# Gelu as a tanh of its cube, its products on GpSimd, normalisations on GpSimd, one list of steps

## The reference

```python
x = L0_attn_x                                    # (8, 1024, 256)
x = x + 0.5 * ffn(layernorm(x))
x = x + attn(layernorm(x))
x = x + 0.5 * ffn(layernorm(x))
# ffn:  16 heads of 16: softmax(q k^T / 16) v, then
z = l2_normalize(z @ Wo)
z = l2_normalize(z @ Wff)
z = gelu(z)                                      # approximate=False
# attn: 8 heads of 32, linear: (q k^T) v without a softmax, then @ w_o.T + b_o
```

## Time and profile before

| | |
|---|---|
| median of 3 runs | 3022.5 us (3019.59 to 3023.07) |
| the profiled execution, own time | 3021.01 us |
| its span | 3019.2 us |
| busy: TensorE, VectorE, ScalarE, GpSimd | 90%, 93%, 91%, 30% |
| mean granted clock of TensorE | 0.983 of full |
| first tile on VectorE | 58.88 us |
| end of the last tile | 2985.0 us |

### The profile page before, as it was taken

The page is one execution under the profiler, slowest core; times in us unless marked ns, Lnnn a source line. Parts: engine busy times, 40 slices in busy tenths (PEclk is TensorE's granted clock), DMA queues, the critical chain, the costliest instruction groups (busy, mean ns, idle before and its releaser), DMA issues.

```text
span 3019.2 us, 88294 instructions
## 1 busy us (share of the span) xinstructions
PE 2728.0 (90%) x36160; PEld 1083.0 (36%) x36160; DVE 2805.7 (93%) x5659; ACT 2734.7 (91%) x5028; POOL 897.4 (30%) x1195
## 2 busy tenths in 40 slices
PE   5989998999989999899998998988989898898987
PEld 2323343334433334343343333333323333332333
DVE  4999999999999999999999999999999999999996
ACT  2999898998999989999898989999999999999997
POOL 3332323323233232331323323232331323233232
PEclk8999999999999999999999999999999999999999
DMA  8223341233412334123331233423223342323332
GB/s 224 54 45 66 57 100 33 52 74 57 90 40 52 77 57 86 42 51 79 58 83 40 52 83 71 85 49 73 54 61 79 71 85 51 73 53 62 76 71 57
DMA packets 155254, 205.53 MB, mean 68 GB/s; under 512 B 34529, under 2 KB 88289, under 8 KB 154722
## 3 DMA queue, kind: packets, MB, share of 16 engines
q1 hardware_dynamic: 154594, 199.37, 31.9%
q0 software_dynamic: 256, 0.52, 0.1%
HBM read 46.66 MB, written 25.17 MB: 24 GB/s over the span
## 4 chain that ended last, share of the span: by engine, by line
PE 32%; DVE 29%; SPq 17%; issue 8%; ACT 8%; POOL 4%; DMA 2%; POOLq 0%; ACTq 0%; DVEq 0%
DVE exp_ring L656 24%; SPq L374 17%; PE ring L770 11%; PE ring L833 9%; PE o_acc L847 9%; ACT exp_ring L580 5%; PE ring L892 2%; DMA kq_stack<-kq_parts 1%; POOL kq_rest L361 1%; POOL kq_parts L365 1%; DVE w_xn L726 1%; ACT w_xn L592 1%; POOL kq_parts L359 1%; POOL kq_parts L363 1%; PE ring L869 1%
## 5 line engine op out<-in xcount | busy, mean ns | idle before, releaser
L580 ACT ACTIVATE exp_ring<-exp_ring,neg_max 128x1024 f32<-128x1024 f32 x2048 | 2344.0, 1146 | 217.1 <-DVE exp_ring L656 209.3
L656 DVE TENSOR_SCALAR_CACHE_REDUCE exp_ring<-ring 128x1024 f32<-128x1024 f32 x2048 | 2407.2, 1216 | 134.7 <-PE ring L833 128.5
L833 PE MATMUL ring<-kq_stack 128*32 128x512 bf16 x16384 | 1155.8, 384 | 161.2 <-DVE exp_ring L656 58.4
L847 PE MATMUL o_acc<-exp_ring,v_scaled 128*32 128x512 f32 x8224 | 1078.9, 600 | 66.0 <-POOL v_scaled L513 41.9
L833 PEld LDWEIGHTS ring<-kq_stack 128*32 128x32 bf16 x16384 | 400.9, 96 | 1089.1 <-issue 338.8
L513 POOL TENSOR_TENSOR v_scaled<-v_now,exp_rsums 128x64 f32<-128x64 f32 x513 | 153.3, 299 | 1708.0 <-DVE exp_rsums L671 1697.8
L580 ACT ACTIVATION_READ_ACCUMULATOR exp_ring<-exp_ring,neg_max 128x1 f32 x2048 | 381.9, 186 | 0.0
L847 PEld LDWEIGHTS o_acc<-exp_ring,v_scaled 128*32 128x32 f32 x8224 | 249.1, 111 | 296.6 <-POOL v_scaled L513 72.1
L770 PE MATMUL ring<-ffn_wo_wowff,o_T 128*32 128x256 f32 x4352 | 258.9, 380 | 3.5 <-DVE exp_ring L656 2.1
L770 PE MATMUL ring<-xn_T,ffn_wqkv 128*32 128x512 f32 x2112 | 256.9, 606 | 3.0 <-DVE exp_ring L656 1.9
L359 POOL TENSOR_TENSOR kq_parts<-kq_stage,zero 128x512 bf16<-128x512 f32 x130 | 143.2, 1101 | 251.3 <-ACT kq_stage L610 149.6
(11 more groups left out here) (102 smaller groups left out, 1298.3 us busy)
## 6 DMA issues: line engine op xcount, KB each, us to landing
kq_stack<-kq_parts SPq DMA_DIRECT2D x2072, 64.0 KB, 2.4
x_post<-x_slots SPq DMA_DIRECT2D x17, 1024.0 KB, 5.7
x_prep<-x_slots SPq DMA_DIRECT2D x16, 1024.0 KB, 8.4
x_slots<-x_post SPq DMA_DIRECT2D x8, 1024.0 KB, 5.6
out<-x_post SPq DMA_DIRECT2D x8, 1024.0 KB, 4.7
x_prep<-in_L_attn_x SPq DMA_DIRECT2D x1, 1024.0 KB, 5.6
exp_ring<-in_L_attn_w_qkv SPq DMA_DIRECT2D x1, 512.0 KB
kq_stack<-kq_parts POOLq DMA_DIRECT2D x8, 64.0 KB, 3.9
```

Of the source, the lines that this page charges most:

```text
L580: nc.scalar.activation(e, e, ACT.Exp, bias=negmax[:, i % NM:i % NM + 1], scale=-1.0, accum_out=sums[:, g % EG, c:c + 1]).then_inc(exp_done, 1)
L656: nc.vector.tensor_scalar(E[:, (g % EG) * HQ + c, :].rearrange("p (b n) -> p b n", b=NB), ps, -1.0, None, ALU.mult, ALU.min, accum_out=neg ...
L833: last = mm(ps[k:k + COLS, n, :], kq[:, 0, c, j * P + k:j * P + k + COLS], kq[:, 1, c, n * BANK:(n + 1) * BANK], start=True, stop=True)
L847: last = mm(O[32 * c:32 * c + 32, n, :], vsc[a][:, g % EG, c, :], E[:, (g % EG) * HQ + c, n * BANK:(n + 1) * BANK], start=(a == 0 and j == ...
```

## The change

The Gelu leaves its table function. y = 4w is made by `gy`, its square `gs`, then `gi` = (square + a constant) times y, `tanh` of it, and `gz` = (tanh + 1) times y; `x1` adds this to the residual (the factor of one half lies in y's scale). It is done in four chunks of 512 columns. In plain phases `gy`, `gs`, `gp` (the added constant as an instruction of its own), `gi`, `xy` (the residual plus y), `gz` and `x1` are all on GpSimd, and only `tanh` on ScalarE. In linear phases `gy` and `x1` are on GpSimd, `gs` and `tanh` on ScalarE, `gi` and `gz` on VectorE. For the last phase's end ("TAIL") `gy`, `gi`, `gz`, `x1` are on VectorE. `xn` and `xn2` go from VectorE to GpSimd, with the negated mean made by a small instruction of its own; only the first `xn` stays on VectorE.

Prologue, phases and epilogue become one sorted list with tables `START`, `PLAIN`, `LINEAR`, `TAIL`; each engine sorts it with offsets of its own (`LEAD`), and semaphore values are counted from these lists. Phase 0 no longer has the steps of an empty phase before. x is read from the input in the first 8 phases, so the copy of the whole input into `x_slots` is gone. The first stack quarter is issued by SyncE (16 DMAs), ScalarE (8) and GpSimd (8) in place of SyncE (24) and GpSimd (8).

```diff
-    WITH_LINEAR = {
-        "u_norm": (28.1,),
-        "w_norm": (31.4,),
-        "gelu": (32.8,),
-        "x1": (36.1, 36.2),
...
+        "LINEAR": {
+            "u_norm": (27,),
+            "w_norm": (29.8,),
+            "form": {"gy": "pool", "gs": "act", "gi": "dve", "gz": "dve", "x1": "pool"},
+            "norm": "pool",
+            "norm2": "pool",
...
+    LEAD = {"sp": {},
+            "pe": {"xt": -0.5},
+            "act": {"qk": 1.0, "u": 1.0, "xt": 0.5, "xt2": 1.5, "gram": 1.0, "G": 0.5, "weights": 0.5},
+            "dve": {"ln2_stats": 0.5, "u_norm": -1.0},
+            "pool": {"w_norm": 0.5, "gy": 1, "xn": -1.0, "u_norm": -0.5}}
...
-                    elif kind == "gelu":
-                        act.wait_ge(norm_step, (p + 1) * 5)
-                        for t in range(NT):
-                            nc.scalar.activation(wb[:, t, 0:D], wb[:, t, 0:D], ACT.Gelu,
-                                                 scale=gsc[:, t:t + 1]).then_inc(gelu_done, 1)
...
+                elif kind == "gy" and form(p)["gy"] == "pool":
+                    pool.wait_ge(norm_step, (p + 1) * 5)
+                    nc.gpsimd.tensor_tensor(w, w, gsc[:, i * CT:(i + 1) * CT].unsqueeze(2).to_broadcast([P, CT, D]),
+                                            ALU.mult).then_inc(gy_done, 1)
+                elif kind == "gp":
+                    pool.wait_ge(gs_done, chunk(p, i))
+                    nc.gpsimd.tensor_scalar(t, t, 1.0, GELU_LIN, ALU.mult, ALU.add).then_inc(gp_done, 1)
...
+                elif kind == "tanh":
+                    act.wait_ge(gi_done, chunk(p, i))
+                    nc.scalar.activation(cube[i % 2][:], cube[i % 2][:], ACT.Tanh, scale=GELU_CUBE).then_inc(tanh_done, 1)
...
+                elif kind == "xn" and table(p - 1)["norm"] == "pool":
+                    pool.wait_ge(rstd_ready, (p + 1) * 2)
+                    nc.gpsimd.tensor_scalar(xp[:, i, :], xp[:, i, :], negm[:, i:i + 1], rstd[:, i:i + 1],
+                                            ALU.add, ALU.mult).then_inc(xn_ready, 1)
```

1233 lines of the change are left out of this document (659 added, 574 removed).

## The result

The changed kernel takes 3161.95 us (median of 4 runs, 3158.29 to 3166.79), the kernel before 3022.78 beside it (3019.59 to 3032.88). The ratio is 1.0452, interval 1.0437 to 1.0467: 139 us slower. I had forecast 3088 (+66) and a range to 3125. The sign was right, the size less than half, and the time lies above the range.

The account below looks back on a forecast made before the run. It took loops through GpSimd's in-order queue and SyncE's DMA issues, not the busy VectorE and ScalarE, as the bound. 38.5 + 32 - 5 - 6 + 7 = +66.5 us gave about 3088, range 3010 to 3125.

Parts of the forecast that it names:

- Start: Before the first tile: SyncE issues 16 stack DMAs instead of 24, so TensorE waits less; -6 us.
- tail: After the last phase: Gelu and x1 in four chunks with VectorE products and some waiting; +7 us.
- Plain phases, second half: First to fourth split on GpSimd's queue: 18 new instructions stretch 37.4 us to 43.1; +5.5 in each of 7 phases, +38.5.
- Plain phases, first half: First 42 places: VectorE gains 2 us from xn, but q and k steps come later; taken as 0, between -2 and +1.5.
- Linear phases: GpSimd's queue and VectorE's products make place 48 7 us late, 3 come back by place 64; +4 in each of 8, +32.
- the loop through SyncE: In plain phases, GpSimd's splits hold back SyncE's stack DMAs, so the 37.4 us stretch goes straight into the phase.
- Phase 15: Counted among the 7 plain phases, with their +5.5 us.
- phase 0: First phase, without the steps of an empty phase: first 42 places -4, ScalarE block in the second half -1; -5 us.
- A: Rival: GpSimd has room, its new instructions cost 0.6 us each and fit its free time; 2996 us, chance 0.17.
- B: Rival: only one-input forms are cheap on GpSimd, plain phases +4.3, linear +1; about 3056 us, chance 0.18.
- C: Rival: everything queues, chunk waits chain up and the shared port costs fully; plain +9, linear +8, 3145 us, chance 0.10.
- The variant of A: On top of A, the ScalarE block (loads and Gelus) is what costs, -5 in each of 15 phases; about 2945 us, chance 0.05.

Follow-up runs that it names:

- e10: Changed kernel with GpSimd's Gelu instructions of plain phases cut to 8 elements a row, order and waits kept; 3127.2 us, ratio 1.0349.
- e14: Changed kernel with all Gelu products, and GpSimd's xn of linear phases, cut to 8 elements a row, waits kept; 3085.6 us, ratio 1.0216.
- e9: Changed kernel with SyncE's output store of plain phases issued behind the next phase's second stack quarter (place 129, not 108); 3164.0 us, ratio 1.0456.
- e12: Changed kernel with GpSimd's gy, x1 and xn of linear phases cut to 8 elements a row, order and waits kept; 3144.3 us, ratio 1.0399.
- e15: e5 with only the linear attention's steps (ln2_stats to y) at the changed kernel's later places; 3096.8 us, ratio 1.0243.
- e5: Changed program with the earlier kernel's table-function Gelu, places, no offsets, and xn, xn2, x1 on VectorE; 3039.0 us, ratio 1.0043.
- e11_small_vector: Changed kernel with VectorE's gi and gz of linear phases cut to 8 elements a row, order and waits kept; 3153.8 us, ratio 1.0430.

## Why the prediction was wrong in size

*Start, tail.* -5.9 for -6 and +9.9 for +7: VectorE waits 0.7 us at each chunk of the tail for ScalarE's square or tanh, and x1 of the last two chunks stands behind it all.

*Plain phases, second half.* Right: the stretch took 43.3 us for 43.1 forecast, with waits that I had not assumed and cheaper one-input forms, two errors that cancel. e10 ties 5.3 us a phase to GpSimd's lengths. From the first of the next quarter's DMAs to the next first tile, another 1.2 us came on top (27.0 for 25.8 in the mean), with the clock at 0.95 in four of six phases; I had nothing there.

*Plain phases, first half* ("I take 0, between -2 and +1.5"). Phase 12 is 3.1 us late at place 64, the mean of phases 9 to 14 is 1.7, just above the range. With the lengths cut the mean is 0.9 in e10 and 2.0 in e14, so they are not shown to be the reason. I looked for the cost in xn on GpSimd's queue. What differs and was not in the forecast: SyncE's store moved behind the first quarter (before, its code issued it ahead of that quarter, now its place is 108 and the quarter's, `stack0`, 91.7), and the clock. e9 puts no more than 0.6 us at place 20 on the store, so the rest stays open.

*Linear phases* ("Behind it nothing falls away. Linear phases: +4 each"). This is the step that failed; the terms ahead of it held in size (place 48 late by 7.0 for 7; 4.8 given back by place 64 for 3). The 7 held partly by luck: I had put it almost all on GpSimd's queue, and with this queue's lengths cut (e12) place 48 is as late as ever, held by VectorE's and ScalarE's waits for each other; only both cuts together (e14) bring it back. I had put the stretch behind place 64 at nothing, and it cost 9.8 us a phase in the mean, 78 of the 95 us: in phase 3, 5.1 between places 64 and 68 and 4.7 between 80 and 100. I had written that "xn2 is gone" from places 48 to 64, booked that as a gain, and did not ask where it, gram, T, VK, G and H had gone: into places 57 to 100. Gram's matmuls stand for 3.5 of the 5.1 us, the lower clock for the rest, and those of VK, G and the first xt2 for the 4.7, where TensorE was full. e15 prices the whole move, without the new Gelu, at 7.5 us a phase, 61 in all; in the changed kernel 4.9 a phase, 39 in all, stay when the lengths are cut (e14). I also gave the loop through SyncE only to plain phases. In a linear one the same 64 DMAs started 5 us late, and TensorE stood 2.40 us ahead of tile 64 before it could begin on gram.

*Phase 15 and phase 0.* Phase 15 was counted as one of seven plain phases, at +5.5; it no longer prepares a next phase and is 6 us shorter. This error of 11.5 us made the miss smaller. Phase 0 lies between 174 and 181 us in the runs of unlike kernels, so that its +2.4 tells nothing.

*The rivals.* A and B fell with the sum. C (3145) came nearest, and half by its own reasons: VectorE does wait 63.5 us in the run for ScalarE's squares. But its plain +9 and linear +8 did not contain the late attention either. The variant of A is added up wrong: -5 in each of 15 phases on top of A's 2996 is 2921; 2945 is about what it gives from 3022. And the row that I set beside the exclusion of VectorE and GpSimd (1.29 against 0.41) is of `xn2`, which has one tensor input and not two; products with two are shown in the last section.

*The signs.* Of those named ahead, the fourth split ended later and SyncE's DMAs started later, by 7 us where I had 5; VectorE's share fell to 87% for 90; the two phase lengths came out at 184 and 202 for 180 and 194, and GpSimd did pause in its stretch.

The pieces, by the phases of the profiled executions, whose spans differ by 144 us: lengths in linear phases 55 (e14), what stays there 39, at the places where TensorE is full with the late linear attention; lengths in plain phases 32 (e10), what stays there 17; start, first and last phase and tail together nothing. The 17 is 2.9 us a phase, and e5, with neither the new Gelu nor the new places, has 2.6 there, so most of it may be the program with its store; this is argued from the sizes and not shown. The runs that build a piece onto the old list give other sizes (attention 61, program 12): the pieces share stalls. How the overlap divides is open, as is the price of the order gi before gs, and what the saved table loads are worth, which no run took by themselves.

## What to carry to other kernels

When an edit makes one step end later, follow every step behind it to its new place and add it to what that engine already does there, before asking what the edit itself costs; here steps that nobody had rewritten cost 39 to 61 us, about as much as all that was written anew cost in the linear phases (55). An engine's low busy share says nothing of how long a queue may be held in the one stretch that a loop runs through. And to price a suspected length, shorten the instruction and keep its waits: moving it to another engine changes two things at once, and here it hid the answer. Cut suspects together as well as alone; one alone can leave the other in the same stall. Last, look at the granted clock of a stretch before its excess is given to instructions.

## What the runs showed of the hardware

GpSimd's tensor_scalar of 128x512, with constants, takes 0.62 us, of 128x256, with two scalars from a tile, 0.55; its tensor_tensor of 128x512 1.04 to 1.28. Of 8 elements a row tensor_tensor takes 0.20 to 0.28, tensor_scalar 0.20 with constants and 0.35 with scalars from a tile (e10, e12). VectorE's products wait out instructions of GpSimd. Those of 8 elements a row in e11_small_vector, the first started just ahead of the end of a GpSimd instruction (L420, from 689.02 for 1.17 us), the next two in the midst of one, and the last beside none:

```profile
690.02 0.19 DVE L719 SCALAR_TENSOR_TENSOR gelu_cube<-gelu_cube,w_xn 128x8 f32<-128x8 f32 x1
...
696.43 0.83 DVE L719 SCALAR_TENSOR_TENSOR gelu_cube<-gelu_cube,w_xn 128x8 f32<-128x8 f32 x1 [5.01 <-ACT gelu_cube L629]
...
704.00 1.35 DVE L719 SCALAR_TENSOR_TENSOR gelu_cube<-gelu_cube,w_xn 128x8 f32<-128x8 f32 x1 [2.02 <-ACT gelu_cube L629]
...
711.04 0.16 DVE L723 SCALAR_TENSOR_TENSOR gelu_cube<-gelu_cube,w_xn 128x8 f32<-128x8 f32 x1
```

GpSimd in the same stretch:

```profile
696.20 1.04 POOL L418 TENSOR_TENSOR kq_parts<-kq_rest,zero 128x512 bf16<-128x512 f32 x1
...
703.24 1.09 POOL L508 TENSOR_SCALAR x_prep<-x_prep,neg_mean,rstd 128x256 f32<-128x256 f32 x2
704.30 1.04 POOL L414 TENSOR_TENSOR kq_parts<-kq_stage,zero 128x512 bf16<-128x512 f32 x1
```

VectorE's product ends at 697.26 and 705.35, GpSimd's instruction at 697.24 and 705.34. The Trainium skill says such a pair excludes each other for the whole length ("SBUF — State Buffer", Who interferes with whom); the trace agrees, with 0.83 us for work of 0.16 to 0.19. The product of 1.35 us began under `xn` (L508) and was still held by the split instruction that GpSimd began 0.30 us after it. What such a product costs is set by what GpSimd is at, not by its own size. So cutting VectorE's products to 8 elements took away only 5.5 us a phase of their 8.9 us of busy time, and won 2.1.
